# Grouped attention layers on one core: one maximum moved ahead of a pair of scores in TensorE's order

## The reference

```python
xn = rmsnorm(x, norm_w)
q = (xn @ wq).reshape(B, T, N_HEADS, HEAD_DIM)          # 16 heads of 32
k = (cond @ wk).reshape(B, S, N_KV_HEADS, HEAD_DIM)     # 4 heads of keys and values
v = (cond @ wv).reshape(B, S, N_KV_HEADS, HEAD_DIM)
qg = q.reshape(B, T, N_KV_HEADS, n_rep, HEAD_DIM)
scores = jnp.einsum('btgrd,bsgd->bgrts', qg, k) * scale
attn = jax.nn.softmax(scores.astype(jnp.float32), axis=-1).astype(q.dtype)
out = jnp.einsum('bgrts,bsgd->btgrd', attn, v).reshape(B, T, N_HEADS * HEAD_DIM)
return residual + out @ wo
```

## Time and profile before

| what | value |
|---|---|
| median of 3 runs | 4220.01 us (4219.65 to 4222.34) |
| the profiled execution | 4216.71 us, its span 4214.9 us |
| granted TensorE clock, mean | 0.989 |
| PE busy | 4068.2 us (97%) |
| PEld busy | 2639.1 us (63%) |
| DVE busy | 2468.1 us (59%) |
| ACT busy | 2074.4 us (49%) |
| POOL busy | 2000.2 us (47%) |
| chain that ended last | PE 43%, DVE 5% |

### The profile page before, as it was taken

How to read it: one execution, slowest core, us unless ns; L and a number is a source line. 1 busy time by engine, 2 the same in 40 slices (tenths; PEclk the granted TensorE clock), 3 DMA queues, 4 the chain that set the end, 5 groups by cost and what they waited for, 6 DMA issues and landing times. The chain is left out here.

```text
span 4214.9 us, 52271 instructions
## 1 busy us (share of the span) xinstructions
PE 4068.2 (97%) x19496; PEld 2639.1 (63%) x19496; DVE 2468.1 (59%) x3453; ACT 2074.4 (49%) x2648; POOL 2000.2 (47%) x1072
## 2 busy tenths in 40 slices
PE   9999999997999999999969999999999999999999
PEld 7888888885556665666544555555555555555555
DVE  3122300013665556555658778777877887788775
ACT  3111211122444445434427666776676677666665
POOL 0000000003565556555626676667666766676666
PEclk9999999998999999999979999999999999999999
DMA  5333522234455445545533333333333333333322
GB/s 185 130 135 135 173 79 83 88 100 118 131 128 134 122 130 130 133 122 133 128 91 84 88 86 86 96 96 97 83 95 90 86 98 93 94 89 88 93 79 65
DMA packets 316070, 452.01 MB, mean 107 GB/s; under 512 B 45176, under 2 KB 117368, under 8 KB 315832
## 3 DMA queue, kind: packets, MB, share of 16 engines
q1 hardware_dynamic: 315832, 448.86, 37.9%
HBM read 217.72 MB, written 102.77 MB: 76 GB/s over the span
## 5 line engine op out<-in xcount | busy, mean ns | idle before, releaser
L1882 DVE TENSOR_REDUCE a_max_cols<-a_ps 128x1 f32<-128x512 f32 x1536 | 1018.1, 673 | 322.6 <-PE a_ps L2014 316.4
L1775 ACT ACTIVATE a_probs<-a_ps 128x1024 f32<-128x1024 f32 x768 | 784.7, 1025 | 602.7 <-PE a_ps L2045 597.4
L2014 PE MATMUL a_ps<-a_k_ops,a_q_ops 96*128 96x512 f32 x1536 | 652.1, 436 | 50.3 <-DVE a_max_cols L1882 33.3
L1684 POOL TENSOR_TENSOR a_sums<-a_probs 128x1024 f32<-128x1024 f32 x192 | 456.1, 2392 | 321.7 <-ACT a_probs L1775 320.5
L1036 DVE TENSOR_REDUCE a_max_cols<-a_ps 128x1 f32<-128x512 f32 x522 | 346.1, 686 | 342.8 <-PE a_ps L1189 342.8
L2014 PEld LDWEIGHTS a_ps<-a_k_ops,a_q_ops 96*128 96x128 f32 x1536 | 291.3, 190 | 396.4 <-DVE a_max_cols L1882 219.1
L2045 PE MATMUL a_ps<-a_q_ops,a_k_ops 128*128 128x512 f32 x1536 | 492.7, 402 | 1.5 <-ACT a_q_ops L1766 0.9
L803 POOL MEMSET a_ident<- 128x128 f32 x1 | 0.2, 204 | 974.9 <-issue 974.9
L1684 POOL TENSOR_TENSOR a_sums<-a_sums,a_probs 128x1024 f32<-128x1024 f32 x192 | 454.0, 2387 | 0.0
L2059 PE MATMUL a_ps<-a_probs,a_v 128*32 128x512 f32 x3072 | 410.1, 606 | 0.9 <-ACT a_probs L1775 0.9
L303 DVE TENSOR_TENSOR cp_c_lo<-cp_raw,cp_c_hi 128x1024 fp32r<-128x1024 f32 x64 | 78.4, 1225 | 527.7 <-ACT cp_c_hi L247 527.7
(11 more groups left out here) (131 smaller groups left out, 7182.0 us busy)
## 6 DMA issues: line engine op xcount, KB each, us to landing
a_k_ops<-k_scratch SPq DMA_DIRECT2D x201, 256.0 KB, 4.1
a_q_ops<-a_qn_hi SPq DMA_DIRECT2D x768, 64.0 KB, 2.0
k_scratch<-cp_out SPq DMA_DIRECT2D x88, 512.0 KB, 2.8
a_q_ops<-a_qn_hi SPq DMA_DIRECT2D x268, 128.0 KB, 2.3
cp_raw<-in_ctx_t SPq DMA_DIRECT2D x64, 512.0 KB, 4.1
x_raw<-out_t SPq DMA_DIRECT2D x25, 1024.0 KB, 7.1
a_q_ops<-a_qn_lo SPq DMA_DIRECT2D x384, 64.0 KB, 2.0
a_x_res<-out_t SPq DMA_DIRECT2D x92, 256.0 KB, 3.1
```

The source lines that it names most:

```text
L1684: pool.tensor_tensor(sums[:, hp], (probs if n < H else sums)[:, hp], probs[:, n], ALU.add)\
L1775: act.activation(probs[:, n], ps[:, 2 * (n % 2):2 * (n % 2) + 2, :], ACT.Exp).then_inc(exped, 1)
L1882: dve.tensor_reduce(max_cols[:, t % 2, col:col + 1], bank(b), AX.X, ALU.max, negate=True)\
L2014: pe.matmul(bank(b), q_ops[0:SHIFT, s, h, q * P:(q + 1) * P], k_ops[0:SHIFT, s, :], start=True, stop=True).then_inc(smax, 1)
```

## The change

One line of TensorE's list moves: maximum 12 now stands right behind the turn and ahead of scores 6, where before it stood behind scores 6 and directly ahead of maximum 13. It does so in all tiles that have a maximum to make there.

```diff
                     maximum(it, t, 11)
                     outputs(it, t, 1, par)
                     turn(*at(it, t + 1))
+                    maximum(it, t, 12)
                     scores(it, t, 6)
-                    maximum(it, t, 12)
                     maximum(it, t, 13)
                     scores(it, t, 7)
                     maximum(it, t, 14)
```

## The result

The changed kernel took 4241.61 us (median of 6 runs, 4236.3 to 4247.87), the kernel before, in the same comparison, 4221.73 (4219.65 to 4226.3). The ratio is 1.0048, with a 95% interval of 1.0035 to 1.0061: 20 us slower, against 9.7 foreseen. The direction was right; the size was out by a factor of two, and beyond the range (4221 to 4237). The profiled execution took 4242.66 us, its span 4240.9.

A forecast was written before the change was run, and what follows sets the result against it. TensorE's list of work was taken to set the time. 16.6 us lost in ordinary tiles less 6.9 gained in first tiles gave +9.7 us, so 4229.7 from a median of 4220.0; the 8-in-10 range was 4221 to 4237.

The forecast's parts named there:

- What bounds the kernel: Grouped layers: TensorE, busy 395.8 of 400 us, sets the time; look for the few places where it stands still.
- the second place: Weight load of the denominators, 0.06 us behind the end of ScalarE's shift: a real wait, and what is lost there stays lost.
- What it delays: Scores 6, ScalarE's chain and the denominators come 0.23 us later in 72 tiles: 16.6 us lost.
- The 0.35 us at maximum 14: TensorE's loss at maximum 14 in ordinary tiles, given back but turned into waiting at scores 0 and outputs 3: costed at nothing.
- What it speeds up in first tiles: VectorE's chain from reduction 12 starts earlier in 23 first tiles, 0.30 us each (bounds 0 and 0.36): 6.9 us gained.
- full lock: First tiles: x_lo fully held by GpSimd's piece would mean no gain there and a sum of +16.6 us.
- The median: The sum of +9.7 us was added to the median of the runs, 4220.0, giving 4229.7.
- A: Rival: the standstill at maximum 14 counts and the shift isn't late; 32 us faster, 4188; chance 0.12.
- B: Rival: only some 0.10 of the 0.23 us delay reaches the denominators; +0.3 us, 4220.3; chance 0.13.
- C: Rival: a maximum behind the turn costs 0.43 us, more than 0.23; +24 us, 4244; chance 0.05.

## Why the prediction was wrong in its size

- *What bounds the kernel; the second place.* Right. The 0.06 us between shift and denominators was a wait, as the distance of 1.01 against 0.88 us between matmuls had said; when the chain was moved either way, the denominators moved with it, until TensorE's own distance of 0.88 was reached.
- *What it delays: 0.23 us in 72 tiles, 16.6 us.* Right in kind, a little small: 0.25, since scores 6 behind a maximum take 0.49 and not 0.46 us. 72 x 0.25 = 18.0 us (71 of the 72 tiles stand ahead of another turn and can be read: 17.4 us in one profile, 17.7 in the other).
- *The 0.35 us at maximum 14 turned into waiting.* Right: scores 0 and outputs 3 now wait for ScalarE, and without ScalarE's chain the gain is there, 22.5 us.
- *What it speeds up in first tiles: 23 x 0.30 = 6.9 us.* This is the step that failed; it measured 0. From a first tile's turn to the next are 21.13 us before and 21.14 after. The head start itself is there, and larger than the 0.36 I had as its bound (0.45), but "the earlier x_lo then misses most of GpSimd's piece" is false. I looked at the x_lo that was slow (x_lo 1) and not at the one that would come to stand beside GpSimd's sum (x_lo 0): it took 0.79 us already, and not the 0.67 that an x_lo takes with GpSimd away. In the kernel before, GpSimd's two sums ahead of the normalising read

```profile
3047.20 4.74 POOL L1684 TENSOR_TENSOR a_sums<-a_sums,a_probs 128x1024 f32<-128x1024 f32 x2
```

and end at 3051.94, 0.25 us behind the start of x_lo 0 (3051.69), which itself ends at 3052.48. So x_lo 0 ends 0.54 us behind the sums; in the changed kernel it starts earlier and ends at 3066.77, 0.55 behind their end at 3066.22. x_lo 1 ends 0.55 us behind the normalising in both (3054.17 and 3053.62; 3068.46 and 3067.91). Moved up, they merely wait longer. In the profiles of both kernels this 0.55 us holds in all first tiles of a pass that have an x_lo behind a running GpSimd piece, 22 of 23. The Trainium skill's rule (GPSIMD Engine Reference, section 8, Key points) speaks of contention between GpSimd and VectorE's instructions with two SBUF inputs, and the trace agrees with it. Taken as a full lock, it gave +16.6, the better sum; that it acts as one here is what the rows show.
- *The median.* I added the sum to a median and left out that the clock differs from run to run. The changed kernel's runs had a little lower mean clock. I put the 2 us between 18 and 20 down to it, which is an estimate: dips add 4.8 and 3.1 us in its two profiles and none in that of before, but the medians were not parted in this way.
- *Rivals.* A (faster) was refuted where it said it decides: the load follows the end of the shift. B failed, all of the 0.23 came through. C failed: behind the turn the maximum took 0.23.

With 18.0 and 0 in place of 16.6 and 6.9 the forecast would have been 4238, and 4240 with the clock. The missing gain in first tiles alone would still lie within the range (4236.6); the other two small terms carry the result over its edge.

## What to carry to other kernels

Where one engine's order is changed to cure a wait, ask which instruction starts the longest chain on another engine, and whether something now stands ahead of it. Here the cured wait of 0.35 us lay ahead of a longer wait and gave nothing back, and the one matmul of 0.23 us now ahead of scores 6 was lost in full. The order on the engine that stands idle at that place is the cheaper place to look: ScalarE was idle for some 3 us there, and with the first half of its shift moved the same edit turned from 20 us lost into 22.5 gained, 30 below the kernel before in all. And a head start on VectorE is worth nothing while the next instruction has two SBUF inputs and GpSimd's piece is still running.

## What the runs showed of the hardware

- A VectorE subtraction of 128x512 with two SBUF inputs takes 0.67 us alone. Started beside a running GpSimd instruction (here always one between SBUF tensors), it ends some 0.55 us behind that one's end, however long it has stood there: 0.79, 1.16, 1.24 and 1.27 us were measured. VectorE's reductions from PSUM beside the same GpSimd pieces keep their 0.68.
- The idle time that the profile shows ahead of a weight load doesn't tell a wait by its length. Behind a group of 32-column matmuls a full-width load that waits for nothing shows 0.84 us (kernel before, at 3001.62, put down to "issue"), and so do the denominators, which wait for the shift. The distance from outputs 3 to the denominators tells: 0.88 us without a wait, 1.01 and 1.21 with one.
- As a standstill of TensorE of 2.6 us ended, or up to 1.5 us later, the granted clock fell to 1.2 GHz for a short while in some executions and not in others (in 22 of 36 such places in the twelve profiles; four dips stand elsewhere). A dip cost 1.5 to 1.65 us in the changed kernel's two profiles (25.54 against 23.97 us from turn to turn in one tile).
